# An early-fusion layer of patches and text: the head on inputs laid out beforehand, expert weights split in place, batch 0 picked in two steps, the softmax ahead of the experts

## The chip, the cores and the metric

The kernel runs on one core of a Trainium2 chip. The metric is the device time of one execution in microseconds (us). A core has TensorE (PE, with its weight loads apart as PEld), VectorE (DVE), ScalarE (ACT), GpSimd (POOL) and the queue engine SyncE (SP), which all run their own instruction streams and meet at semaphores. 16 DMA engines move data between memory and SBUF.

## What is computed

```python
patches = [x and four copies shifted by 8 pixels]          # 32 x 36 patches of 3840 values
h = ((patches - mu) * rsqrt(var + eps) * gamma + beta) @ W.T + b     # W: 192 x 3840
h = concatenate([h, txt], axis=1)                          # 32 x 164 x 192
n = layernorm(h)
k, v, q = n @ w_key.T, n @ w_value.T, n @ w_query.T        # 8 heads of 64
k0, v0, g0 = k[0], v[0], sigmoid(n @ w_gate.T)[0]          # of batch 0 alone
for t in sequence:                                         # retrieved, then written
    out_t = q_t @ fw;  fw = 0.95 * fw + 0.1 * g0_t * outer(k0_t, v0_t)
h = h + n + out @ w_out.T
n = layernorm(h);  xf = rmsnorm(n) * norm_w                # 5248 tokens
p = softmax(xf @ router_w.T);  top 2 of 8 experts
y = sum over them of p_e * down_e(silu(gate_e xf) * (up_e xf))       # 384 wide
h = h + n + y
```

All arrays are float32. An image is 96 x 96 with three channels, so it has 6 x 6 patches.

## The kernel before

The kernel is one block in which each engine's queue is written out by hand in Python; semaphores are named after what is ready (wait_ge). A tile is 4 sequence positions of 32 batches, 128 rows; there are 41 tiles, 9 of them patches, and the residual hres holds all of them in SBUF. The program has these stages.

*Preparation.* SP's queue (L358) loads W, beta, gamma, the image in 12 pieces of 32 partitions, and the text. Attention weights come through ScalarE's queue (L434). TensorE transposes w_out (L690), forms for each head the products gT (key by query weights) and hT (value by output weights) (L701), 192 columns each, and transposes W (L717). VectorE multiplies W by gamma and folds columns that shifted copies share. GpSimd copies image rows into strips, TensorE transposes them (L738), VectorE copies them to imgT (L1048).

*Patches* (L750). Nine patches, each 24 products of 128 x 128 by 193 columns; the 193rd column gives the sum of the pixels. An fp32 product is two instructions on TensorE in the trace. ScalarE's squares (L471, L474), before all patches in its queue, give the variance; VectorE finishes each token (L1072).

*Batch 0.* Its normed row x0T comes from a round trip through DMA; the gates, keys and values of all heads follow (L773, L794), with evictions L523 and L1142; the gates reach their partitions by eight small DMAs.

*Chunk loop.* Eleven chunks of 16 positions (4 tiles). Per chunk TensorE makes the transposes turn (L782), rows (L802, L804), scores (L814), the read-out of the state (L820) and of the chunk itself (L824), and the state's update (L835). ScalarE copies the transposed tokens out (xT_out, L518), computes std2 (L545), and norm2 (L555 to L559), which writes the rows that are scattered. VectorE adds the residual, takes the statistics and top 2 and gives each token a place. GpSimd scatters each tile twice (L662) to the place of its expert in memory. Between them stand *units* of expert weights: TensorE transposes a piece (L852, L853, L858), ScalarE writes its high half rounded (high, L572 and L576), VectorE the rest (low, L1238 and L1244). 20 units stand in the loop, 24 after it. At the end VectorE computes the table of slots (L1266 to L1288).

*Experts.* 89 slots of 128 rows each: SP loads the rows of a slot (L413) when all scatters are done, TensorE runs a pipeline of transposes and products, GpSimd scatters each result.

*Tail.* Results come back in groups of four tiles (L346), ScalarE takes the softmax's exp (L630), VectorE adds two results per tile (L1343), stores leave by both queues (L356).

```python
def unit(n):                       # before: 12 down units, then 32 of gate and up
    k = n - NE * FC // 2
    return None if k < 0 else (k // 4, k // 2 % 2, k % 2)
for n in range(LOOP_UNITS, UNITS): # VectorE, after the table
    low(n)
```

## Time and profile before

| what | us |
|---|---|
| median of 3 runs | 672.92 (671.53 to 672.93) |
| profiled execution, its own time | 671.68 |
| its span | 669.9 |
| preparation and patches | 0 to 164.1 |
| batch 0, to the chunk loop | 164.1 to 207.2 |
| chunk loop, table, last units | 207.2 to 338.0 |
| experts | 338.0 to 625.9 |
| tail | 625.9 to 669.9 |

The rows further down are from the views of the trace: windows give each engine's busy time in a stretch with the number of instructions in brackets, PEclk the clock granted to TensorE as a share of the full 2.4 GHz (0.50 is 1.2 GHz), and GB/s what the DMA engines moved. A timeline's row gives the start, the duration, the engine, the line and operation, then output<-input, and in brackets the idle time ahead of it and what released it. The ends of products are modelled, so that the spacing of starts tells more than a duration.

### The profile page before, as it was taken

How to read it: one execution, taken by the hardware profiler on the slowest of the kernel's cores; microseconds unless marked ns; L12 is line 12 of the kernel's file. 1: busy time of each engine (PE TensorE's matmuls, PEld its weight loads, DVE VectorE, ACT ScalarE, POOL GpSimd, SP SyncE). 2: the span in 40 equal slices, each digit the busy share in tenths (PEclk: the TensorE clock that was granted, in tenths of full speed). 3: DMA queues.
4: the chain of work that ended last, by engine and by line, in shares of the span. 5: the costliest groups of instructions: out<-in, count | busy, mean ns of one | idle time of the engine just before them, and what ended most of it. 6: DMA issues, size and time to landing. Idle time of an engine off the chain costs nothing.

```text
span 669.9 us, 13234 instructions
## 1 busy us (share of the span) xinstructions
PE 541.2 (81%) x3330; PEld 500.7 (75%) x3331; DVE 402.7 (60%) x1310; ACT 305.2 (46%) x718; POOL 198.5 (30%) x293
## 2 busy tenths in 40 slices
PE   0079998997589999984679999999999999999000
PEld 0067688997487877873379999999999999999000
DVE  4590617666414777788956566566566566565197
ACT  0035992222623667767644444444444444444100
POOL 0001510000000577777403333333333333333100
PEclk9999998999599999998789999999999999999655
DMA  9999700000861122222312222222222222221695
GB/s 201 236 170 187 139 0 1 7 1 0 204 187 42 54 81 78 79 79 85 106 38 78 69 73 79 69 74 78 69 77 74 69 79 72 69 80 48 214 371 155
DMA packets 85236, 64.87 MB, mean 97 GB/s; under 512 B 42501, under 2 KB 81897, under 8 KB 84825
## 3 DMA queue, kind: packets, MB, share of 16 engines
q1 hardware_dynamic: 67160, 39.93, 26.8%
q0 software_dynamic: 8208, 16.95, 7.2%
...
q14 instruction: 15, 0.11, 0.1%
...
## 4 chain that ended last, share of the span: by engine, by line
PE 69%; DVE 14%; ACT 7%; DMA 4%; issue 3%; ACTq 2%; POOL 0%; POOLq 0%; SPq 0%; DVEq 0%
PE pair L750 9%; PE bank L946 5%; PE bank L942 5%; PE bank L944 5%; PE bank L945 5%; PE bank L943 5%; PE bank L953 4%; PE pair L820 4%; DVE hres L1343 4%; ACT sqjunk L471 4%; PE bank L962 4%; PE pair L962 4%; DMA bet<-in_L_tok_ln_beta 3%; PE pair L931 3%; PE bank L701 3%
## 5 line engine op out<-in xcount | busy, mean ns | idle before, releaser
L662 POOL DMA_INDIRECT disp<-xf,posu x82 | 79.8, 973 | 154.3 <-ACT xf L559 130.2
L674 POOL DMA_INDIRECT ydram<-ysb,dnow x89 | 87.3, 981 | 69.4 <-POOL dnow L671 67.1
L1308 DVE TENSOR_TENSOR hh<-sg,bank 128x384 f32<-128x384 f32 x89 | 49.3, 554 | 93.4 <-ACT sg L613 93.4
L613 ACT ACTIVATE sg<-bank 128x384 f32<-128x384 f32 x89 | 43.7, 491 | 111.5 <-PE bank L946 111.5
L750 PE MATMUL pair<-wcT,imgT 128*128 128x193 f32 x432 | 73.4, 331 | 3.8 <-DVE tmp L1063 3.8
L750 PEld LDWEIGHTS pair<-wcT,imgT 128*128 128x128 f32 x432 | 72.4, 193 | 4.1 <-issue 4.1
L942 PE MATMUL bank<-wa,xh 128*128 x178 | 67.7, 380 | 0.0
L946 PE MATMUL bank<-wa,xl 128*128 x178 | 60.3, 339 | 0.0
L944 PE MATMUL bank<-wa,xl 128*128 x178 | 60.2, 338 | 0.0
L945 PE MATMUL bank<-wa,xh 128*128 x178 | 60.0, 337 | 0.0
L943 PE MATMUL bank<-wa,xh 128*128 x178 | 60.0, 337 | 0.0
L671 POOL COPY dnow<-dest 128x1 uint32 (+1 forms) x89 | 16.5, 186 | 123.9 <-DVE ysb L1318 123.9
L1311 DVE TENSOR_TENSOR htl<-bank,hth 128x384 fp32r<-128x384 f32 x89 | 48.9, 550 | 0.9 <-ACT hth L616 0.9
L962 PE MATMUL pair<-wd,hth 128*128 x135 | 44.5, 380 | 0.4 <-DVE htl L1311 0.4
L953 PE MATMUL bank<-ident,hh 128*128 128x128 f32 x267 | 43.6, 272 | 0.6 <-DVE htl L1311 0.6
L962 PE MATMUL bank<-wd,hth 128*128 x132 | 43.6, 380 | 0.0
L616 ACT CAST hth<-bank 128x384 fp32r<-128x384 f32 x89 | 42.4, 476 | 0.8 <-PE bank L953 0.8
L931 PE MATMUL pair<-ident,xs 128*128 128x128 f32 x178 | 34.4, 275 | 4.0 <-DVE wa L1244 3.0
L953 PEld LDWEIGHTS bank<-ident,hh 128*128 128x128 f32 x267 | 34.6, 140 | 3.8 <-DVE hh L1308 0.8
L1304 DVE TENSOR_TENSOR xl<-pair,xh 128x256 fp32r<-128x256 f32 x89 | 37.2, 418 | 0.4 <-ACT xh L610 0.4
L652 POOL COPY strip<-img 128x512 f32<-128x512 f32 x24 | 13.7, 606 | 77.5 <-DMA img<-in_x 62.8
L820 PE MATMUL pair<-nst,xT 96*128 96x208 f32 x164 | 36.3, 343 | 0.0
...
## 6 DMA issues: line engine op xcount, KB each, us to landing
...
```

Of the source, the lines that this page charges most:

```text
L662: pool.indirect_dma_start(disp, bass.IndirectOffsetOnAxis(ap=posu[c % XBUF][:, 2 * j + k:2 * j + k + 1], axis=0), xfd[c % XBUF][:, j, :], None
L674: pool.indirect_dma_start(ydram, bass.IndirectOffsetOnAxis(ap=dnow[b][:], axis=0), ysb[b][:], None).then_inc(s_ys[b], 16)
L750: ins = pe.matmul(bank[5 + p % 2][:, 0:193], imgT[:, 2 * i + dr, j + s, c, :], wcT[:, k, :], start=(k == 0), stop=(k == 23))
L820: pe.matmul(o, xT[c % 2][:, m, P * j:P * j + P], nst[c % 2][:, m, :], start=(m == 0), stop=False)
L931: ins = pe.transpose(bank[5][:, P * m:P * m + P], xs[b][:, P * m:P * m + P], ident[:])
L942: pe.matmul(acc, xh[o][:, 0:P], high, start=True, stop=False)
L943: pe.matmul(acc, xh[o][:, 0:P], low, start=False, stop=False)
L944: pe.matmul(acc, xl[o][:, 0:P], high, start=False, stop=False)
L945: pe.matmul(acc, xh[o][:, P:2 * P], rest, start=False, stop=False)
L946: ins = pe.matmul(acc, xl[o][:, P:2 * P], rest, start=False, stop=True)
L953: ins = pe.transpose(bank[4][:, P * c:P * c + P], hh[b][:, P * c:P * c + P], ident[:])
L962: pe.matmul(bank[6 + o][:, 0:2 * D], hth[o][:, P * c:P * c + P], wd[:, both], start=(c == 0), stop=False)
```

## The change

All inputs are laid out by numpy before the launch: the pixels as imgT wants them, a second copy of them in four horizontal bands for the squares, W cut into 30 pieces of 128 x 192, the attention weights transposed, the text by partitions, gate, up and down weights transposed. No transposes of weights or images are left on TensorE, no strips on GpSimd, no border zeroes and no head products. VectorE multiplies the 24 pieces of W by gamma and adds six shared ones. TensorE multiplies all 30 by gamma and beta to get two row sums (L711), spreads them over the partitions (L733), and runs the patches over four banks (L727). The squares move between the patches on ScalarE's queue. Bands 2 and 3 reuse the buffers of 0 and 1.

Keys and values of batch 0 come in two steps. First the projections of the text positions (L742, between patches 7 and 8) and their products with query or output weights (L757). Then the patches' positions are picked from hres by products with a one-hot selection scaled by the rstd (L807, L811), projected, and multiplied (L765). The gates are picked on VectorE.

There are 4 down units in the head and 24 of gate and up in the loop, in 22 turns, none after it. The loaded piece lies where its low half will: ScalarE writes the high half from it, VectorE subtracts. The second norm of chunk 0 moves to the end of chunk 0 in ScalarE's queue. The softmax stands ahead of the experts. Results lie in memory by partition, and the first loads of the tail have 1, 1 and 2 tiles.

```diff
+LOADS = (0, 1, 2, 4, 8, 12, 16, 20, 24, 28, 32, 36, 40, 41)
...
+        def turn_units(t):
+
+            n = UNITS - DOWN_UNITS
+            return range(DOWN_UNITS + max(0, t - 1) * n // (TURNS - 1), DOWN_UNITS + t * n // (TURNS - 1))
...
-            sp.dma_start(wraw[:], W.rearrange("(m p) f -> p m f", p=DH)).then_inc(s_wraw, 16)
-            sp.dma_start(bet[:], beta.partition_broadcast(DH)).then_inc(s_bet, 16)
-            sp.dma_start(gam[:], gamma.partition_broadcast(DH)).then_inc(s_gam, 16)
...
+                sp.dma_start(wraw[:, 15 * i:15 * i + 15, :], W[:, 15 * i:15 * i + 15, :]).then_inc(s_wraw[i], 16)
+            for i in range(2):
+                sp.dma_start(imgT[:, 2 * i:2 * i + 2], pixels[:, 2 * i:2 * i + 2]).then_inc(s_img[i], 16)
+            for i in range(2):
+                sp.dma_start(band[i][:], bands[:, i]).then_inc(s_band[i], 16)
+            sp.dma_start(imgT[:, 4:6], pixels[:, 4:6]).then_inc(s_img[2], 16)
+            sp.dma_start(hres3[:, PTILES:TILES, :], text).then_inc(s_txt, 16)
...
+            sp.wait_ge(s_row, 1)
...
+                sp.dma_start(x0[32 * q:32 * q + 32, :], text[32 * q]).then_inc(s_x0, 16)
+            sp.dma_start(imgT[:, 6:8], pixels[:, 6:8]).then_inc(s_img[3], 16)
+            sp.dma_start(aw[:], attn_w).then_inc(s_attw, 16)
+            for i in range(2):
+                sp.wait_ge(s_sq, 12 + 9 * i)
+                sp.dma_start(band[i][:], bands[:, 2 + i]).then_inc(s_band[2 + i], 16)
+                if i == 0:
+                    sp.dma_start(wd4[:, :, 1, :].bitcast(F32), down_w).then_inc(s_rawd, 16)
+
...
+            for e in range(NE):
+                sp.dma_start(wa5[:, e, 1].bitcast(F32), gu_w[0:P, e]).then_inc(s_rawm[e], 16)
+            sp.wait_ge(s_kv, 4 * NH)
+            for r in range(2 * NE):
+                if r >= RING:
+                    sp.wait_ge(s_lo, DOWN_UNITS + 3 * ((r - RING) // 2) + (r - RING) % 2 + 2)
+                for half in range(2):
+                    sp.dma_start(ring[r % RING][64 * half:64 * half + 64, :], gu_w[P:D, r // 2, r % 2]).then_inc(s_rawr[r % RING], 16)
...
+                lines = (0, 1) if i == 0 else (i + 1,)
+                if j == 0:
+                    for b in lines:
+                        act.wait_ge(s_band[b], 16)
+                for b in lines:
+                    square(sqjunk[:], band[b % 2][:, :, :, 16 * j:16 * j + 32], 12 * j + 3 * b + 1)
+                square(sqjunk[:, :, 0:8, 0:16], band[i % 2][:, :, 8:16, 16 * j + 8:16 * j + 24], 12 * j + 3 * i + 2)
+                square(sqjunk[:, :, 0:8, 0:16], band[(i + 1) % 2][:, :, 0:8, 16 * j + 8:16 * j + 24], 12 * j + 3 * i + 3)
+
...
+                    if k == 0:
+                        act.wait_ge(s_rawm[e], 16)
+                        ins = nc.scalar.activation(wa5[:, e, 0], wa5[:, e, 1].bitcast(F32), ACT.Copy, scale=nwab[:, 0:1])
+                    else:
+                        r = 2 * e + k - 1
+                        act.wait_ge(s_rawr[r % RING], 32 * (r // RING + 1))
+                        ins = nc.scalar.activation(wa5[:, e, 2, k - 1], ring[r % RING][:], ACT.Copy, scale=nwab[:, 1:2])
...
                 if c + 1 < CHUNKS:
                     xT_out(c + 1, 0)
-                if c + 1 < CHUNKS:
-                    high(2 * c)
+                for n in turn_units(2 * c):
+                    high(n)
                 if c + 1 < CHUNKS and nt(c + 1) > 2:
                     xT_out(c + 1, 1)
-                if c:
+                if c > 1:
                     norm2(c - 1)
                 if c + 1 < CHUNKS:
                     state_out(c + 1)
-                    high(2 * c + 1)
+                for n in turn_units(2 * c + 1):
+                    high(n)
                 if c + 2 < CHUNKS:
                     rows(c + 2)
                 if c:
                     add_norm2(c - 1)
                 std2(c)
+                if c == 0:
+                    norm2(0)
             norm2(CHUNKS - 1)
             add_norm2(CHUNKS - 1)
...
+            act.wait_ge(s_w, 1)
+            nc.scalar.activation(top8[:, 0:8 * TILES], top8[:, 0:8 * TILES], ACT.Exp).then_inc(s_exp, 1)
+            nc.scalar.preload_act_table_set("silu_and_others")
...
+            pe.wait_ge(s_par, 16)
+            for k in range(WCOLS):
+                if k % 15 == 0:
+                    pe.wait_ge(s_wraw[k // 15], 16)
+                pe.matmul(bank[4][0:2, 0:D], gb[:, k, :], wraw[:, k, :], start=(k == 0), stop=False)
+            pe.wait_ge(s_cst, 16)
+            pe.wait_ge(s_bias, 16)
+            pe.matmul(bank[4][0:2, 0:D], cst[0:1, C_ONE:C_ONE + 2], biasr[:], start=False, stop=True).then_inc(s_row, 1)
 
...
+                if p >= 4:
+                    pe.wait_ge(s_patout, p - 3)
...
+            for p in range(1, 7):
+                patch(p)
+            pe.wait_ge(s_x0n, 1)
+            for m in range(2):
+                ins = pe.transpose(bank[2][0:DH, P * m:P * m + P], x0n[:, DH * m:DH * m + DH], ident[:])
+            ins.then_inc(s_x0t, 1)
+            patch(7)
...
+            def pick(tiles):
+                a, n = tiles[0], len(tiles)
+                pe.matmul(x0sel[:, :, a:a + n, :], onesf[:, 0:DH], selr[:, 1, a:a + n].unsqueeze(1).to_broadcast([P, 2, n, TQ]),
+                          start=True, stop=False)
+                for t in tiles:
+                    for m in range(2):
+                        ins = pe.matmul(x0sel[:, m, t, :], hres3[:, t, DH * m:DH * m + DH], selr[:, 0, t, :],
+                                        start=False, stop=(t == tiles[-1] and m == 1))
+                return ins
+
+            pe.wait_ge(s_rsel, 1)
...
+            text_kv(1, 0)
+            pe.wait_ge(s_head, 1)
+            pe.wait_ge(s_patout, 9)
+            for which in range(2):
+                for hp in range(4):
+                    ins = project(head_bank[which][:, HEAD_S * hp:HEAD_S * hp + HEAD_S], (wkT, wvT)[which], hp, 0, HEAD_S)
+                ins.then_inc(s_k0, 1)
+            text_kv(1, 1)
+            for m in range(2):
+                ins = pe.matmul(bank[3][:, 0:SPAD], wgR[:, m, :], x0T[:, m, :], start=(m == 0), stop=(m == 1))
+            ins.then_inc(s_g8, 1)
+            turn(0, 0)
+            text_kv(1, 2)
+            text_kv(1, 3)
+            for which in range(2):
+                pe.wait_ge((s_k0head, s_v0head)[which], 1)
+                pe.wait_ge(s_vvout, 6 + 2 * which)
+                for hp in range(4):
+                    head_kv(which, hp)
 
...
+            def low(n):
+                v.wait_ge(s_hi, n + 1)
+                if unit(n) is None:
+                    raw = wd4[:, 6 * n:6 * n + 6, 1, :]
+                    ins = v.tensor_tensor(raw, raw.bitcast(F32), wd4[:, 6 * n:6 * n + 6, 0, :].bitcast(F32), ALU.subtract)
+                else:
+                    e, k = unit(n)
+                    if k == 0:
+                        raw = wa5[:, e, 1]
+                        ins = v.scalar_tensor_tensor(out=raw, in0=raw.bitcast(F32), scalar=nwab[:, 0:1],
+                                                     in1=wa5[:, e, 0].bitcast(F32), op0=ALU.mult, op1=ALU.subtract)
+                    else:
+                        both = wa5[64:P, e, 2, k - 1, :]
+                        ins = v.scalar_tensor_tensor(out=both, in0=ring[(2 * e + k - 1) % RING][64:P, :], scalar=nwab[64:P, 1:2],
+                                                     in1=both.bitcast(F32), op0=ALU.mult, op1=ALU.subtract)
+                ins.then_inc(s_lo, 1)
+
+            for p in range(9):
...
+            t4 = top8[:].rearrange("p (c j e) -> p c j e", j=4, e=8)
+            t3 = top8[:, 0:8 * TILES].rearrange("p (n e) -> p n e", e=8)
+            st.link(v.tensor_tensor(t4, t4, rs[:, :, 1, :].unsqueeze(3).to_broadcast([P, CHUNKS, 4, 8]), ALU.mult))
+            st.link(v.tensor_copy(esum[:], t3[:, :, 0]))
+            v.tensor_tensor(t3, t3, esum[:].unsqueeze(2).to_broadcast([P, TILES, 8]), ALU.subtract).then_inc(s_w, 1)
+            v.wait_ge(s_exp, 1)
+            st.link(v.tensor_reduce(esum[:], t3, AX.X, ALU.add))
+            st.link(v.reciprocal(esum[:], esum[:]))
+            st.link(v.tensor_tensor(wts[:].rearrange("p (n k) -> p n k", k=2), t3[:, :, 0:2],
+                                    esum[:].unsqueeze(2).to_broadcast([P, TILES, 2]), ALU.mult))
...
-    c[:, C_DEST:C_DEST + TILES] = 2 * (P * np.arange(TILES)[None] + p[:, None])
+    c[:, C_DEST:C_DEST + TILES] = 2 * (np.arange(TILES)[None] + TILES * p[:, None])
...
+        "pixels": quads.reshape(P, CH, 8, 8, 4, 16).transpose(5, 3, 2, 4, 1, 0).reshape(P, 8, 4, CH, P),
+        "bands": quads.reshape(P, CH, 4, 16, 64).transpose(0, 2, 1, 3, 4),
+        "text": txt.reshape(B, TILES - PTILES, TQ, D).transpose(2, 0, 1, 3).reshape(P, TILES - PTILES, D),
+        "patch_w": pieces(inputs["L0_tok_W"]),
```

TensorE's queue in the preparation before, behind the transposes of w_out: the last head product and the first transposes of W (wraw), which go on for nine more such groups.

```order
L701 MATMUL bank<-woT,wv 96x192 [waits product_out]
L701 MATMUL bank<-woT,wv 96x192
L717 MATMUL bank<-ident,wraw 128x96 [waits product_out,patch_weights_ready]
L717 MATMUL bank<-ident,wraw 128x96 x7
L717 MATMUL bank<-ident,wraw 128x96 [waits wT_out]
L717 MATMUL bank<-ident,wraw 128x96 x3
```

TensorE's queue from its start now, with row sums (of wraw, the pieces of W) and the first patches:

```order
L711 MATMUL bank<-wraw,qpar 2x192 [waits patch_weights_in0,params_in]
L711 MATMUL bank<-wraw,qpar 2x192 x14
L711 MATMUL bank<-wraw,qpar 2x192 [waits patch_weights_in1]
L711 MATMUL bank<-wraw,qpar 2x192 x14
L714 MATMUL bank<-biasr,cst 2x192 [waits bias_in,consts_in]
L727 MATMUL bank<-wcT,imgT 128x193 [waits pixels_in1,pixels_in0,patch_weights_ready]
L727 MATMUL bank<-wcT,imgT 128x193 x23
L733 MATMUL bank<-rowsb,onesf 128x384 [waits rows_masked]
L738 MATMUL bank<-ident,rw_66 96x8 [waits router_centred,pool_constants]
L738 MATMUL bank<-ident,rw_66 96x8
L727 MATMUL bank<-wcT,imgT 128x193 x24
L727 MATMUL pair<-wcT,imgT 128x193 x24
```

The transposes and products are gone; 30 products and the bias stand ahead of patch 0, and the spreading of the row sums and the router's transposes behind it.

ScalarE's queue around the ends of chunks 0 and 1 before (xT is a turn's copy, sq the std2, xf what norm2 writes, wd and wa high halves, nst the state, crow and arow the rows):

```order
L545 ACTIVATE sq<-mv_138,cst 128x4 [waits var2]
L546 ACTIVATE sq<-mv_138,cst 128x4
L518 COPY xT_150<-bank 96x2x256 [waits state_mm,xT_mm]
L572 CAST wd<-bank 128x2x192 [waits expertT_mm]
L518 COPY xT_150<-bank 96x2x256 [waits state_mm,xT_mm]
L555 COPY xf_86<-cst 128x4x2 [waits rstd2]
L557 COPY xf_86<-idxf 128x4
L559 ACTIVATE xf_86<-hres,bb,rs 128x192 x4
L539 COPY nst_143<-bank 96x2x200 [waits state_mm]
L572 CAST wd<-bank 128x2x192 [waits expertT_mm]
```

And now:

```order
L586 ACTIVATE sq<-mv_128,cst 128x4 [waits var2]
L587 ACTIVATE sq<-mv_128,cst 128x4
L596 COPY xf_78<-cst 128x4x2 [waits rstd2]
L598 COPY xf_78<-idxf 128x4
L600 ACTIVATE xf_78<-hres,bb,rs 128x192 x4
L560 COPY xT_140<-bank 96x2x256 [waits state_mm,xT_mm]
L501 ACTIVATE wa<-ring_62,qpar 128x384 [waits raw_rest_in0]
L560 COPY xT_140<-bank 96x2x256 [waits state_mm,xT_mm]
```

norm2(0) went ahead of both xT copies that TensorE's turns of chunk 2 wait for, and a high half from a ring buffer stands between them.

VectorE at the end of the table before:

```order
L1286 TENSOR_SCALAR slotf<-slotf 128x91 [waits dve_steps]
L1287 CAST tab<-slotf 128x91 [waits dve_steps]
L1288 CAST tab<-slotf 128x91
L1244 SCALAR_TENSOR_TENSOR wa<-bank,nwab,wa 128x384 [waits expert_high,dve_steps]
L1244 SCALAR_TENSOR_TENSOR wa<-bank,nwab,wa 64x384 [waits expert_high]
```

And now (top holds the logits, wts the weights):

```order
L1330 CAST tab<-slotf 128x91
L1335 TENSOR_TENSOR top_136<-top_136,rs 128x352 [waits dve_steps]
L1336 COPY esum<-top_136 128x41 [waits dve_steps]
L1337 TENSOR_TENSOR top_136<-top_136,esum 128x328 [waits dve_steps]
L1339 TENSOR_REDUCE esum<-top_136 128x41 [waits softmax_exp]
L1340 RECIPROCAL esum<-esum 128x41 [waits dve_steps]
L1341 TENSOR_TENSOR wts<-top_136,esum 128x82 [waits dve_steps]
L1349 SCALAR_TENSOR_TENSOR dest<-xs_155,slotf 128x1 [waits xsT_mm,dve_steps]
```

The 24 low halves are gone from there, and the softmax's six operations, with a wait for ScalarE's exp, stand ahead of the first slot's operations.

## Rows read from the trace of the kernel before

**Rows 1.** Windows by stage: from:to, length, busy time of each engine, PEclk, DMA, GB/s.

```profile
0.00:103.10 103.10, 59.17 (x299) 49.53 (x300) 46.85 (x82) 50.02 (x68) 14.90 (x33) 1.00 0.87 152
103.10:164.10 61.00, 60.35 (x360) 59.22 (x360) 39.13 (x172) 14.55 (x37) 0.00 (x0) 0.97 0.01 3
164.10:207.20 43.10, 29.85 (x172) 26.25 (x172) 14.73 (x62) 16.70 (x38) 0.00 (x0) 0.84 0.62 168
207.20:338.00 130.80, 110.79 (x632) 88.54 (x632) 102.71 (x461) 87.02 (x217) 79.82 (x82) 0.95 0.22 72
338.00:625.90 287.90, 281.04 (x1869) 277.15 (x1869) 169.12 (x448) 135.19 (x357) 103.81 (x178) 0.99 0.25 71
625.90:669.90 44.00, 0.00 (x0) 0.00 (x0) 30.12 (x85) 1.76 (x2) 0.00 (x0) 0.50 0.84 275
```

**Rows 2.** Windows of 2 us, loading W and loading results.

```profile
14.00:16.00 2.00, 0.00 (x0) 0.00 (x0) 0.00 (x0) 0.00 (x0) 0.00 (x0) 1.00 1.05 223
...
638.00:640.00 2.00, 0.00 (x0) 0.00 (x0) 1.97 (x7) 0.00 (x0) 0.00 (x0) 0.50 1.06 373
```

**Rows 3.** TensorE's timeline: head products at the start, and the patches.

```profile
41.63 1.16 PE L701 MATMUL bank<-wq,wk 64*96 64x192 f32 x3
42.59 1.16 PE L701 MATMUL bank<-woT,wv 64*96 64x192 f32 x3
...
124.56 39.53 PE L750 MATMUL pair<-wcT,imgT 128*128 128x193 f32 x240
```

**Rows 4.** Groups by line: count, then busy us, mean ns of one, idle before.

```profile
L471 ACT ACTIVATE sqjunk<-img 128x3072 bf16<-128x3072 f32 x9 | 24.9, 2764 | 0.3
...
L996 DVE TENSOR_TENSOR wq<-wq,wqm 128x768 f32<-128x768 f32 x1 | 1.0, 959 | 0.0
```

**Rows 5.** TensorE: a group of head products (timeline), and the rows' narrow products (lines).

```profile
187.73 1.36 PE L794 MATMUL pair<-x0T,hT 96*96 96x176 f32 x8
...
L804 PE MATMUL bank<-rwsc,valsT 96*128 96x8 f32 x44 | 5.9, 243 | 0.0
```

**Rows 6.** Timelines of the loop: GpSimd, VectorE, ScalarE, SP's queue, TensorE.

```profile
222.45 1.14 POOL L662 DMA_INDIRECT disp<-xf,posu  x1 [129.28 <-ACT xf L559]
...
316.59 1.25 POOL L662 DMA_INDIRECT disp<-xf,posu  x1 [0.30 <-issue]
...
318.14 1.60 POOL L662 DMA_INDIRECT disp<-xf,posu  x1 [0.30 <-issue]
...
326.37 0.96 POOL L662 DMA_INDIRECT disp<-xf,posu  x1 [0.30 <-issue]
...
316.09 0.92 DVE L1277 TENSOR_TENSOR tabf<-cst,ct 128x728 f32<-128x728 f32 x1
...
317.99 0.92 DVE L1280 TENSOR_TENSOR tabf<-tabf,ct 128x728 f32<-128x728 f32 x1
...
321.58 15.47 DVE L1244 SCALAR_TENSOR_TENSOR wa<-bank,nwab,wa 128x384 fp32r<-128x384 f32 x24
...
220.32 0.58 ACT L518 COPY xT<-bank 96x512 f32<-96x512 f32 x1 [1.86 <-PE bank L782]
...
221.00 1.86 ACT L559 ACTIVATE xf<-hres,bb,rs 128x192 f32<-128x192 f32 x4
...
329.85 0.37 SPq L413 DMA_DIRECT2D xs<-disp  x1
...
338.01 0.41 PE L931 MATMUL pair<-ident,xs 128*128 128x128 f32 x2 [2.97 <-DVE wa L1244]
```

**Rows 7.** Timelines of the tail: ScalarE's queue and VectorE.

```profile
625.85 7.89 ACTq L346 DMA_DIRECT2D yall<-ydram  x5
...
636.84 29.70 DVE L1343 SCALAR_TENSOR_TENSOR hres<-yall,wts,hres 128x192 f32<-128x192 f32 x82
```

**Rows 8.** Windows late in the chunk loop, columns as in the first group.

```profile
297.00:307.00 10.00, 7.57 (x49) 6.81 (x46) 8.55 (x43) 6.61 (x18) 7.56 (x9) 1.00 0.23 79
307.00:317.00 10.00, 3.93 (x17) 3.08 (x17) 7.87 (x42) 7.01 (x21) 7.56 (x9) 0.73 0.23 79
```

859 lines of the change are left out of this document (417 added, 442 removed).

## The prediction

> **What bounds the kernel now.** The windows by stage come first [rows 1]. The experts' stage, 338.0 to 625.9, takes 287.9 us with TensorE busy 281.0, and the change touches no instruction in it. The time to be won lies around it: 207.2 us before the chunk loop, 130.8 from its start to the first expert slot, 44.0 behind the last slot. The profiled execution took 671.68 us for a span of 669.9, so 1.8 us lie outside the span; the median of the runs shown, 672.92, is 0.2% above it.
>
> In the first 103.1 us TensorE is busy 59.2, though the transfers run at 152 GB/s on average: the loads come in narrow shapes, and behind them come the folding of W, the head products and the transposes. The patches then run one after another, busy 60.35 of 61.00. In the 43.1 us after them TensorE is busy 29.9. In the loop GpSimd issues its 82 scatters in an unbroken row, the first at 222.45, the last at 326.37 [rows 6], so one every (326.37 - 222.45 - 0.93)/81 = 1.27 us, the 0.93 being two stretched ones; eight of them make 10.1 us a chunk. The last scatter ends at 327.33, the first slot's load is issued at 329.85, but TensorE begins at 338.01, since 24 units of expert weights (15.47 us of VectorE) stand after the table [rows 6]. In the tail the loads are issued at 625.85 and the first addition runs at 636.84 [rows 7].
>
> **Head, to the loop's start (call it L; 207.2 before).** *Loads.* W goes out first on SP's queue, two pieces of 1.47 MB over 128 partitions with 11.5 KB in a row. Bounds on their rate: 223 GB/s, the old W over 96 partitions, and 373, the results over 128 partitions [rows 2]. I take 370, the row with the same partitions and long rows. With 3.2 us until data flows (my estimate from the first window), piece 0 is there at 7.2, piece 1 at 11.2, pixels for the first three patches at 19.2.
> *Row sums.* TensorE starts cold with 30 matmuls of 192 columns, two instructions each. At the start of the old kernel's work such an instruction took 0.96/3 = 0.32 us, against 39.53/240 = 0.165 for 193 columns in mid-run [rows 3]; so these run at 1.2 GHz, the lower of the two clocks. Price: 30 x 0.656 = 19.7, at the other clock 9.9. They are ahead of patch 0 in TensorE's queue, so it waits for them, not for the weights: VectorE's fold (four operations of 128 x 1152, each 1.5 x 0.96 by the row of 768 [rows 4], and twelve of 192 columns) is ready at 17.7. Patch 0 starts at 7.2 + 19.7 + 1 = 28.
> *Patches.* 9 x 48 x 0.165 = 71.1; the first partly at the low clock +2; row spread, x0's two transposes and queueing +1.5; the 32 projection instructions between patches 7 and 8 +3.5 at 0.11 each. They end at 106. Gone are 96 image and 48 W transposes, the products and the strips. The squares, of which the larger pieces alone took 24.9 us ahead of the patches [rows 4], now lie beside them: one patch costs ScalarE at most two pieces of 1536 elements and two of 384, 0.9 ns an element by 2764/3072, 3.5 us under 7.9.
> *To L.* Key products over the text 7.0 (32 instructions x 0.11 = 3.5, and as much for the squares, projections and additions still queued on ScalarE and VectorE); picks of batch 0, 22 matmuls = 44 instructions x 0.135 by the eight-column row, 5.9 [rows 5]; value products 4.0; head projections 4.3; gate 0.6; turns 0.9; 32 head products, 64 instructions, 7.7 (0.12 each, under the 0.135 of the eight-column row since their spans overlap; 1.36/8 = 0.17 for 176 columns is the upper bound [rows 5]); evictions, rows and scores 4.6. Sum 35, against 43.1 before, with the transfer of the gate through memory and x0's round trip gone. **L = 141**, 66 us earlier.
>
> **Loop, L to the first slot.** Before, the first scatter stood at L + 15.2 and the slot's data could have been used at L + 125.3: the last scatter's end and 5.2 more. The 24 units kept it to L + 130.8; moving them into the loop gives at most 5.5 back. Three things take from it.
> *The second norm of chunk 0* now stands ahead of the copies xT(2,0) and xT(2,1). Before, it stood behind them, and ScalarE waited 1.86 us for the second at 220.32, so norm 0 began at 221.00 [rows 6]. Its four activations (1.86) and their wait for VectorE now stand ahead of a copy that TensorE's turn(2,1) waits for. Chunk 0 scatters some 2.4 us sooner, chunk 1's chain comes some 3.5 later. Bounds -2.4 and +3.5; I take +1.9, what GpSimd is starved once it has used its lead.
> *Splitting units.* The low halves (8 of 128 x 768, 16 of 64 x 384) took one operand from PSUM; now both come from SBUF. In this trace the two table operations with both big operands in SBUF, 316.09 and 317.99, are exactly those under which scatters took 1.25 and 1.60 us instead of 0.96 [rows 6]; the reductions between them stretched none. A 0.96 us operation that starts anywhere in the 1.27 us period holds up the next scatter by some 0.3 on average, one of 0.5 us by 0.1: 8 x 0.3 + 16 x 0.1 = **+4.0**. Bounds 0 and their whole length, 8 x 0.96 + 16 x 0.5 = 15.7; the two stretches measured (0.29 and 0.64) hold me near the low end. The Trainium skill, "SBUF — State Buffer", section "Who interferes with whom", says that a VectorE operation with both inputs in SBUF locks GpSimd's reads out for as long as it lasts. By that rule these units cost GpSimd time in a stage that GpSimd bounds; the trace agrees in the two scatters, and by the rule at its hardest the loop would end some 12 us later than in my sum.
> *TensorE* loses its expert transposes; its 10.3 us a chunk fall to some 8.3, hidden under GpSimd's 10.1. The softmax (under 3 us on VectorE, its exp on ScalarE) hides behind the last scatters, which end 5.6 us after the table. If that cover went, it would cost those 3.
> Sum: 125.3 + 1.9 + 4.0 = **131.2**.
>
> **Experts** 287.9, as before. **Tail.** A first load of one tile lets additions start at +3.2 instead of +11.0 [rows 7]: landing about 2 us, issue the rest. Gone from the front are the exp's table load and the softmax's four operations. Then 82 additions 29.3, waits for the growing pieces 1.5, the last store 3.9: 37.9, take **38**. It can't go under 12.1 MB / 373 GB/s = 32.4 [rows 2].
>
> **Sum:** 141 + 131.2 + 287.9 + 38 = 598.1, and 1.8 outside: **600**.
>
> **Rivals.**
> *A, the loads stay slow.* For it: 223 GB/s at 14 to 16 and 152 over the head. Against it: those rows are 96 partitions and runs of 224 bytes. At 225 GB/s the third band, queued behind text, pixels and attention weights, lands at 88; patch 3's squares wait for it, and patch 6 waits for one of four banks. L = 153, time 613.
> *B, TensorE starts fast.* The row sums take 9.9, patch 0 waits for its weights and pixels at 20: 592. Against it: the first rows behind an idle stretch ran at 1.2 GHz [rows 3].
> *C, the loop is free:* no stretched scatters and norm 0 early, the slot at L + 126: 595.
> *D, the clock falls in the loop.* With the expert transposes gone TensorE idles. It held the full clock at 76% busy (297 to 307), and fell to 0.73 at 39% (307 to 317) [rows 8]. At some 80% it should hold; where it doesn't, a chunk's 8.3 us become 16 and pass GpSimd's 10.1 until it rises again. I price it at 1 us a chunk: 610.
> *Slower than before: the loads throttle everything.* 19 MB must come in ahead of L, of which 69 us of work can't be covered: L = 69 + 19/r. It decides at L = 213, r = 132 GB/s, where the time reaches 673. The head's average is 152, with descriptors fifty times shorter, so it is remote: 675 to 690.
> *The change doesn't do what it says:* small first loads and the early softmax bring nothing, since a hidden DMA limits the tail: that is 605 and lies in the range; that all of it brings nothing has 1 in 100.
>
> **How the numbers follow.** Forecast 0.54 (its own range 592 to 608), A 0.15, B 0.11, C 0.10, D 0.07, slower 0.02, nothing 0.01. The low end, 585, is B with C and 2 us of head; the high end, 616, is A with a few us of locked scatters. About 0.2% is what a measurement of this kernel can tell from no change. Faster 0.97, same 0.01, slower 0.02.
>
> **What would show it.** First rows on TensorE: 0.33 us an instruction from about 7 us on; patch 0 at 28; the patches 7.9 apart to 106 with no wait for squares; the loop's first rows at 141. GpSimd's first scatter at L + 13, its last at L + 125, with some twenty stretched ones under the low halves. First slot at L + 131. First addition 3 us behind the last store. I am wrong if wraw lands after 10, if a patch waits for a band, if ScalarE's queue holds up the key products by more than 4 us, or if DMA is over 95% busy in the tail while additions wait.

## The result, and the profile after

The changed kernel takes 593.44 us (median of 4 runs, 592.90 to 593.84) against 672.76 for the kernel before (4 runs), a ratio of 0.882 (95% interval 0.881 to 0.884). The forecast was 600. The profiled execution took 593.84 for a span of 592.1. Its windows by stage, in the same columns and with the same cuts as [rows 1], with one more cut at the first patch:

```profile
0.00:20.63 20.63, 12.70 (x63) 5.80 (x64) 9.79 (x19) 0.00 (x0) 1.36 (x10) 1.00 0.92 373
20.63:103.47 82.84, 78.65 (x470) 77.53 (x470) 53.39 (x230) 54.51 (x116) 0.00 (x0) 0.96 0.50 189
103.47:133.66 30.19, 28.38 (x242) 25.25 (x241) 11.34 (x41) 12.84 (x30) 0.00 (x0) 0.72 0.37 124
133.66:265.59 131.93, 88.47 (x493) 75.00 (x492) 96.92 (x447) 81.45 (x202) 81.94 (x82) 0.87 0.30 91
265.59:554.40 288.81, 282.15 (x1869) 278.18 (x1869) 167.98 (x445) 133.49 (x356) 104.15 (x178) 0.98 0.26 71
554.40:592.10 37.70, 0.00 (x0) 0.00 (x0) 29.04 (x82) 0.00 (x0) 0.00 (x0) 0.50 0.88 321
```

The chunk loop starts at L = 133.66 instead of 207.2: that is 73.5 of the 77.8 us that the span lost. The loop to the first slot takes 131.9 (130.8 before), so its end brought nothing, the experts 288.8 (287.9), the tail 37.7 (44.0). What the prediction rests on in the head is in these rows of TensorE, VectorE and ScalarE (timeline: start, busy, engine, line, operation, count, idle before and what ended it):

```profile
7.79 12.29 PE L711 MATMUL bank<-wraw,qpar 128*2 128x192 f32 x60 [7.79 <-DMA wraw<-in_patch_w]
20.63 8.14 PE L727 MATMUL bank<-wcT,imgT 128*128 128x193 f32 x48
89.39 6.28 PE L742 MATMUL bank<-x0T,aw 96*128 96x128 f32 x32 [4.19 <-DVE x0T L1161]
113.32 7.06 PE L742 MATMUL bank<-x0T,aw 96*128 96x48 f32 x32
...
10.54 0.19 DVE L994 COPY wcT<-cst 128x24 f32<-128x24 f32 x1 [10.54 <-DMA cst<-in_consts]
81.20 2.63 DVE L1116 TENSOR_TENSOR wd<-wd 128x1152 fp32r<-128x1152 f32 x2 [6.27 <-ACT wd L492]
...
77.11 1.48 ACT L464 ACTIVATE sqjunk<-band 128x1536 bf16<-128x1536 f32 x1 [2.70 <-DMA band<-in_bands]
...
80.02 2.21 ACT L492 CAST wd<-wd 128x1152 fp32r<-128x1152 f32 x2
```

The row sums (L711) begin 7.8 us in and take 12.3: the first 16 of their 60 instructions start 0.32 us apart, the others 0.16. The fold waits until 10.5 for a copy of constants ahead of it in VectorE's queue (L994), and ends together with the sums. TensorE idles 4.2 us for x0T (L1161), behind the casts of the down units (L492, L1116). Those casts stand behind squares for which ScalarE itself waits 2.70 us, until the fourth band has landed (L464, 77.11). The projections after it run at the lower clock:

```profile
7.00:13.00 6.00, 5.21 (x18) 2.21 (x19) 2.46 (x3) 0.00 (x0) 0.00 (x0) 1.00 1.02 429
13.00:20.00 7.00, 7.00 (x44) 3.50 (x42) 6.86 (x15) 0.00 (x0) 0.00 (x0) 1.00 1.01 427
89.00:95.50 6.50, 6.11 (x32) 6.14 (x33) 4.81 (x10) 2.77 (x4) 0.00 (x0) 0.57 0.01 3
112.00:124.00 12.00, 12.00 (x60) 10.87 (x62) 2.77 (x8) 2.32 (x7) 0.00 (x0) 0.50 0.15 58
```

These are windows in the head (columns as above; PEclk, DMA share and GB/s last). The loads run at 427 to 429 GB/s, where 370 was taken from [rows 2]. The Trainium skill, "DMA: Bandwidth & Descriptors", section "Where 436 GB/s comes from", gives 435 GB/s as the ceiling of the ports into SBUF and some 358 for what memory gives a core, and says that the second binds transfers from memory. The trace lies just under the first figure and above the second, and the measurement decides. The last line shows 12 us between patches and loop at 0.50 of the clock, the lower of the two levels.

In the loop, of GpSimd, ScalarE, TensorE and VectorE:

```profile
147.61 1.12 POOL L683 DMA_INDIRECT disp<-xf,posu  x1 [145.43 <-ACT xf L600]
162.78 0.96 POOL L683 DMA_INDIRECT disp<-xf,posu  x1 [5.19 <-ACT xf L600]
181.64 1.34 POOL L683 DMA_INDIRECT disp<-xf,posu  x1 [0.31 <-issue]
...
146.15 1.86 ACT L600 ACTIVATE xf<-hres,bb,rs 128x192 f32<-128x192 f32 x4
147.91 0.56 ACT L560 COPY xT<-bank 96x512 f32<-96x512 f32 x1
...
161.47 1.86 ACT L600 ACTIVATE xf<-hres,bb,rs 128x192 f32<-128x192 f32 x4
...
148.62 0.61 PE L779 MATMUL bank<-ident,hres 128*96 128x128 f32 x4 [2.89 <-ACT xT L560]
...
265.59 0.69 PE L946 MATMUL pair<-ident,xs 128*128 128x128 f32 x2 [20.40 <-DMA xs<-disp]
...
144.52 1.01 DVE L1121 SCALAR_TENSOR_TENSOR wa<-wa,qpar 128x768 fp32r<-128x768 f32 x1
181.13 1.01 DVE L1121 SCALAR_TENSOR_TENSOR wa<-wa,qpar 128x768 fp32r<-128x768 f32 x1
```

GpSimd scatters chunk 0 and then stands for 5.19 us, where it stood for nothing before [rows 6]: chunk 1's rows come late. Norm 0 (L600) runs ahead of the copy xT (L560), and TensorE's turn waits 2.89 us for that copy. One scatter, at 181.64, takes 1.34 us under a low half on VectorE (L1121, 181.13).

In the tail (SP's queue and VectorE) the loads go out at 554.40 and the first addition runs 3.41 us later, against 10.99 in [rows 7]:

```profile
554.40 3.34 SPq L366 DMA_DIRECT2D yall<-ydram  x7
...
557.81 1.53 DVE L1383 SCALAR_TENSOR_TENSOR hres<-yall,wts,hres 128x192 f32<-128x192 f32 x4 [6.85 <-DMA yall<-ydram]
```

### The profile page after: what moved, and what is told of

Same layout as the page of the kernel before. It is cut to its first block, busy times and chain, and to the rows that moved or that the text cites. A ratio compares the mean times of both kernels' runs of the same rounds, so it can differ in the third digit from the quotient of the medians.

```text
span 592.1 us, 12735 instructions
## 1 busy us (share of the span) xinstructions
PE 490.3 (83%) x3132; PEld 461.8 (78%) x3133; DVE 368.5 (62%) x1263; ACT 282.3 (48%) x703; POOL 187.5 (32%) x270
## 4 chain that ended last, share of the span: by engine, by line
PE 61%; DVE 18%; DMA 10%; ACT 5%; issue 3%; POOL 2%; SPq 1%; DVEq 0%; POOLq 0%
DMA hres<-in_text 6%; PE bank L961 5%; PE bank L959 5%; PE bank L958 5%; PE bank L957 5%; PE bank L960 5%; PE bank L968 5%; DVE hres L1383 4%; PE bank L977 4%; PE pair L977 4%; PE pair L863 4%; PE pair L946 3%; PE pair L867 3%; ACT sqjunk L464 2%; PE bank L742 2%
## 5 line engine op out<-in xcount | busy, mean ns | idle before, releaser
L683 POOL DMA_INDIRECT disp<-xf,posu x82 | 81.9, 999 | 176.4 <-ACT xf L600 151.5
L692 POOL COPY dnow<-dest 128x1 uint32 (+1 forms) x89 | 16.6, 186 | 119.0 <-DVE ysb L1368 118.9
L946 PE MATMUL pair<-ident,xs 128*128 128x128 f32 x178 | 34.9, 278 | 21.4 <-DMA xs<-disp 20.4
L727 PE MATMUL bank<-wcT,imgT 128*128 128x193 f32 x240 | 40.2, 327 | 0.1
L727 PEld LDWEIGHTS bank<-wcT,imgT 128*128 128x128 f32 x240 | 39.3, 189 | 0.6 <-DVE zrow L1012 0.5
L642 ACT CAST xh<-pair 128x256 fp32r<-128x256 f32 x89 | 33.5, 376 | 11.2 <-PE pair L946 11.2
L863 PE MATMUL pair<-nst,xT 96*128 96x208 f32 x164 | 38.0, 356 | 0.2 <-ACT nst L580 0.2
L946 PEld LDWEIGHTS pair<-ident,xs 128*128 128x128 f32 x178 | 20.8, 143 | 22.0 <-DMA xs<-disp 21.9
```

The source lines that it names most:

```text
L683: pool.indirect_dma_start(disp, bass.IndirectOffsetOnAxis(ap=posu[c % XBUF][:, 2 * j + k:2 * j + k + 1], axis=0), xfd[c % XBUF][:, j, :], None
L727: ins = pe.matmul(bank[PATCH_BANK[p % 4]][:, 0:193], imgT[:, 2 * i + dr, j + s, c, :], wcT[:, k, :], start=(k == 0), stop=(k == 23))
L863: pe.matmul(o, xT[c % 2][:, m, P * j:P * j + P], nst[c % 2][:, m, :], start=(m == 0), stop=False)
L946: ins = pe.transpose(bank[5][:, P * m:P * m + P], xs[b][:, P * m:P * m + P], ident[:])
```

## The experiments

The total came near the forecast, but four terms looked off: the start, the stretch between patches and loop, norm 0, and the locked scatters. Twelve runs followed on three chips. On the chip of e1 to e4 and on that of the four g kernels every kernel was slower, the one before too (717.4 and 718.1); the extra time lies in the chunk loop, where VectorE and ScalarE stand still together for several us. In g0, the changed kernel itself, the timeline of the two has rows such as these, in which the profile names nothing on the core as releaser:

```profile
186.46 0.22 DVE L1271 TENSOR_TENSOR ohm<-oh,pair 128x64 f32<-128x64 f32 x1 [4.13 <-remote]
186.62 0.58 ACT L560 COPY xT<-bank 96x512 f32<-96x512 f32 x1 [3.36 <-remote]
```

So from those chips I read the head, the first two chunks and the tail, and compare kernels of one chip. The third chip (before 673.15), that of e5, e6, h1 and h2, has none of it. All of them, from their traces ("+" counts from L; scatter 9 is chunk 1's first; the column of times gives the number of executions in brackets):

| kernel | time (n) / before on that chip | patch 0 | patches end | L | scatter 1 | scatter 9 | L to slot | slot to tail | tail |
|---|---|---|---|---|---|---|---|---|---|
| after | 593.44 (4) / 672.76 | 20.63 | 103.54 | 133.66 | +13.95 | +29.1 | 131.93 | 288.81 | 37.7 |
| e1 | 632.53 (4) / 717.37 | 21.36 | 104.14 | 134.35 | +14.69 | +28.3 | 169.53 | 289.15 | 37.7 |
| e2 | 631.23 (4) / 717.37 | 21.71 | 97.73 | 132.63 | +13.96 | +32.2 | 169.57 | 289.14 | 37.6 |
| e3 | 632.73 (1) | 21.5 | 100.71 | 134.33 | +13.15 | +31.6 | 170.33 | 288.34 | 37.9 |
| e4 | 636.32 (1) | 21.83 | 102.21 | 136.26 | +15.94 | +34.6 | 171.83 | 288.76 | 37.8 |
| g0 | 642.11 (2) / 718.05 | 21.49 | 100.54 | 140.61 | +15.92 | +34.5 | 172.04 | 288.65 | 37.6 |
| g1 | 627.49 (2) / 718.05 | 21.81 | 100.42 | 134.00 | +14.68 | +26.0 | 167.54 | 289.38 | 37.4 |
| g3 | 631.56 (1) | 21.52 | 103.51 | 133.62 | +13.15 | +31.4 | 169.55 | 288.99 | 37.6 |
| g9 | 629.79 (1) | 18.69 | 102.4 | 132.64 | +13.95 | +31.9 | 169.45 | 288.45 | 37.5 |
| e5 | 605.54 (1) | 21.61 | 100.65 | 140.72 | +16.10 | +31.7 | 134.98 | 288.58 | 39.5 |
| e6 | 595.05 (1) | 21.43 | 100.53 | 132.62 | +13.96 | +29.1 | 132.61 | 288.44 | 39.6 |
| h1 | 586.61 (3) / 673.15 | 18.71 | 94.70 | 132.02 | +14.69 | +25.4 | 127.22 | 287.89 | 37.8 |
| h2 | 591.71 (4) / 673.15 | 18.73 | 94.72 | 142.37 | +16.84 | +27.5 | 128.48 | 288.41 | 37.7 |

**Norm 0 behind the copies: e1, and g1 on the other chip.** The edit of both:

```diff
-                if c > 1:
+                if c:
                     norm2(c - 1)
...
-                if c == 0:
-                    norm2(0)
```

> The changed kernel with one part undone: the second norm of chunk 0 stands again behind the two xT copies of chunk 2, as in the kernel before. Theory: in the changed kernel GpSimd is starved for 4.9 us at 157.6 to 162.8 since ScalarE's four activations and their wait for VectorE hold up TensorE's turn of chunk 2 (idle 2.89 us at 148.6). Then this gap goes, chunk 0's first scatter comes some 2 us later (L + 16), chunk 1's no later than L + 26, and the first slot starts 3 us sooner: L + 129, span 589. Rival: the gap comes from the units of expert weights, for whose high half VectorE waits 3.18 us at 149.1 ahead of its residual. Then the gap stays about as long, and the first slot starts at L + 132 or later, span 592.

> The second norm of chunk 0 back behind the two xT copies, beside a control on the same chip. Theory as before: TensorE's wait of 2.9 us and most of GpSimd's 4.9 us without work in chunk 1 go, the first scatter comes 1 to 2 us later, and the first slot starts 2 to 3 us sooner after L than in the control. Rival: the units hold VectorE up just as long, and the first slot comes no sooner than in the control.

In e1 the first scatter comes 0.73 us later than in e2 of the same chip, and chunk 1's first one at L + 28.3 instead of L + 32.2, not at the L + 26 that was expected: one of the standstills (3.09 us of VectorE) lies ahead of it. In g1 the row of scatters goes nearly straight on into chunk 1:

```profile
160.01 0.96 POOL L681 DMA_INDIRECT disp<-xf,posu  x1 [0.69 <-issue]
```

That is L + 26.0, against L + 31.9 in g9 and L + 34.5 in g0, the kernels of that chip that keep norm 0 ahead. So the mechanism stands. In e1's total nothing of it is to be seen (L to slot 169.53, against 169.57 in e2), since the standstills of that chip use up any lead; in g1 it is 1.9 us against g9 and 4.5 against g0, but g9 and g0, which have the same loop, differ by 2.6 among themselves. The size is read from h1 below, which has other edits too; no kernel with this edit alone ran on a chip without standstills.

**The down units one patch later: e2.**

```diff
-                if 4 < p < 7:
+                if 5 < p < 8:
                     ...
-                        high(2 * (p - 5) + n)
+                        high(2 * (p - 6) + n)
```

(and the same for the low halves on VectorE).

> The changed kernel with its four down units one patch later in ScalarE's and VectorE's queues, so that the copy x0T on VectorE has none of them ahead. Theory: TensorE's wait of 4.19 us ahead of the projections at 89.4 comes from the low halves, which VectorE waits for (6.27 us) ahead of patch 5's and 6's work; with it goes the fall of the clock to 0.57 in the projections (6.3 us where 3.5 would do). Patches end at 97 instead of 103.5, and L is 6 to 7 us earlier: span 586. Rival: the fourth band, which ScalarE waits for until 77.1, sets x0T's time, or the units now hold up the picks: at most 1 us is gained, span 591.

The wait for x0T and the fall of the clock behind it go: the patches end at 97.7, six us earlier than in after and three to six than in the others of its chip. But L is 132.6, only some 1.7 earlier than e1 and e3, and e6, with the head of after, has the same 132.6; so a gain at L isn't clear of the spread. Behind the patches TensorE now waits there (timeline):

```profile
101.88 0.53 PE L757 MATMUL bank<-k0T,aw 64*96 64x128 f32 x1 [3.10 <-ACT keysT L537]
```

ScalarE and VectorE have the last patch's evictions and the last down units ahead of the keys, and keysT is late; the products behind it start 0.21 us apart, twice the 0.11 of those before the wait. The cause of the first wait is confirmed, and the gain was mostly or wholly handed to the next wait. The other traces say the same without an edit: in e3, g0, g1, e5 and e6, whose heads are that of after, the projections took 3.81 us at the full clock instead of 6.28, the patches ended at 100.4 to 100.7, and the wait for keysT was 2.5 us instead of 0.4.

**Low halves of one column: e3, and g3 on the other chip.** Both leave out all but one column of each low half, so the experts work with wrong weights.

```diff
-                        ins = v.scalar_tensor_tensor(out=raw, in0=raw.bitcast(F32), scalar=nwab[:, 0:1],
+                        ins = v.scalar_tensor_tensor(out=raw[:, 0, 0:1], in0=raw[:, 0, 0:1].bitcast(F32), scalar=nwab[:, 0:1],
```

> The changed kernel, in which the 24 low halves of gate and up are computed for one column only; the rest of them is left as loaded. It prices what VectorE's operations with both operands in SBUF cost GpSimd's scatters. The prediction had 4.0 us for it. The trace of the changed kernel shows four stretched scatters ahead of the table's (0.38, 0.66, 0.36 and 0.09 us over 0.96), 1.5 us in all. By that these four stretches go, those under the table's two operations and the softmax stay (0.64, 0.63, 0.17), and the first scatter comes 1 us sooner since the first low half stood ahead of chunk 0's scaling: first slot at L + 129.5 instead of L + 131.9. By the prediction's price it would be L + 127.

> The 24 low halves of gate and up for one column only (the rest stays as loaded), beside a control on the same chip. By the four stretches that the trace shows ahead of the table: scatters stretched by 1.5 us less than in the control, first scatter 1 us sooner, first slot 2 to 3 us sooner after L. By the prediction's price of 4.0 us for the stretches: 5 us sooner.

The first scatter comes at L + 13.15 in both, 0.8 earlier than in after, e2, e6 and g9, which have full low halves: a whole 1.01 us one (L1121 at 144.52, above) stood ahead of norm 0's scales. Time over 0.96 us, summed over all scatters, is 1.01 in g3 and 1.33 in g0; none of g3's lies under a low half, and of g0's only 0.2. In after, four scatters of the 82 are longer under low halves, by 0.38, 0.66, 0.36 and 0.09: 1.5 us, where 24 such operations run. In the four runs of the third chip it is 6 to 9 scatters and 1.7 to 2.3 us. What the low halves cost the loop in all can't be told from e3 and g3, since both ran where engines stand still (169.55 and 170.33, inside the spread of the others).

**Fewer narrow products in batch 0's picks: e4.** It leaves out all but the last tile's selections, so keys and values of batch 0 are wrong.

```diff
-                for t in tiles:
+                for t in tiles[-1:]:
```

> The changed kernel without 14 of the 18 narrow products that pick batch 0's patches out of hres (the last tile of each pick stays), so keys, values and gates of the patch positions are wrong. The trace shows TensorE's clock at 0.50 from 109 to 124.6 though it is busy all the time, with the head projections at 7.06 us. Theory: products of four columns make the clock fall, and without them it stays at 1.00 to the loop: 4.7 us of picks and some 7 us of slow clock go, L = 122, span 580. Rival: the clock falls for the gaps at 104.6 and 108.9 or since the projections before ran in a cold stretch; then only the 4.7 us go, L = 129, span 587.

```profile
106.00:109.00 3.00, 1.42 (x17) 1.33 (x16) 1.98 (x14) 2.01 (x4) 0.00 (x0) 1.00 0.96 358
...
130.00:133.00 3.00, 3.00 (x6) 1.59 (x7) 0.00 (x0) 0.64 (x2) 0.00 (x0) 0.50 0.46 132
```

The windows (columns as above) show TensorE idle for half of the time in which the picks stood, and the clock down at 130, when it had long risen in after. L is 136.3, not earlier. So the clock falls there without most of the narrow products too; with them gone there is idle time in their place. Whether it would hold with neither, the run doesn't tell.

**Loads of four tiles first: e5. Softmax behind the experts: e6.**

```diff
-LOADS = (0, 1, 2, 4, 8, 12, 16, 20, 24, 28, 32, 36, 40, 41)
+LOADS = (0, 4, 8, 12, 16, 20, 24, 28, 32, 36, 40, 41)
```

> The changed kernel with its first tail load of four tiles again instead of 1, 1 and 2. Theory: the first addition waits for 786 KB instead of 197 KB while the other queue's load runs beside it: 3.4 us from the tail's start become 5.5 to 6, the additions behind wait no more, and the tail takes 39 to 40 us instead of 37.7. Rival: the tail's end is set by the transfers, which go on at 370 GB/s either way: 37.7.

> The changed kernel with the softmax behind the experts again. Theory: ScalarE issues its six loads (2.9 us), loads the exp's table (1.28) and takes the exp (0.48), then VectorE's reduction, reciprocal and product follow (1.2): first addition at 6.4 us from the tail's start instead of 3.4, tail 40.5 instead of 37.7. The loop's end is unchanged (the softmax was behind the last scatters). Rival: the additions catch up, since later ones wait for loads anyway: tail under 38.5.

In e6 exp moves behind load_results on ScalarE, and the softmax's operations stand on VectorE between the experts and the additions. First e5, then e6, timelines of the tail:

```profile
564.28 2.96 SPq L366 DMA_DIRECT2D yall<-ydram  x6
...
570.35 4.74 DVE L1383 SCALAR_TENSOR_TENSOR hres<-yall,wts,hres 128x192 f32<-128x192 f32 x13 [9.50 <-DMA yall<-ydram]
```

```profile
553.67 3.50 SPq L366 DMA_DIRECT2D yall<-ydram  x7
...
556.83 1.28 ACT L660 ACT_TABLE_LOAD   x1 [7.60 <-issue]
...
559.89 5.53 DVE L1383 SCALAR_TENSOR_TENSOR hres<-yall,wts,hres 128x192 f32<-128x192 f32 x15
```

The first addition starts 6.07 us behind the issue with loads of four, 6.22 with the softmax there, 3.41 in after. The tails are 39.5, 39.6 and 37.7: 1.8 and 1.9 us each, less than the 2.7 and 2.8 by which the start moves, since additions that start early wait later for the growing pieces (0.79 us in after). Either one alone holds the start back to +6, so each gives its gain only with the other; the kernel with neither wasn't run. What brings the tail from 44.0 to 39.5 wasn't tried apart (the results lie in memory in another layout).

**A warm start: g9.** TensorE multiplies ones for 16 products before W lands, and the copy of constants moves behind the fold.

```diff
+            pe.wait_ge(s_pool, 1)
+            for k in range(16):
+                pe.matmul(bank[3][:, 0:P], onesf[:], onesf[:], start=True, stop=True)
```

> The changed kernel with 16 products of ones on TensorE from 1 us on, ahead of the row sums (their result is used nowhere), and with VectorE's copy that waits for the constants (10.5 us) behind its folding of W instead of ahead of it. Theory: both the row sums (12.3 us, 18 instructions at half clock) and the fold (ready at 20.35) end together and set patch 0; with the clock up from the start the sums take 9.9 us and end at 17.9, and the fold, from 8 us on, ends at 18: patch 0 at 18.2 instead of 20.6, and the whole 2.4 us shorter. Rival: the pixels or the second piece of W come later than 18, or the half clock of the start isn't cured by these products: patch 0 at 20 or later.

```profile
1.04 5.23 PE L709 MATMUL bank<-onesf 128*128 128x128 f32 x32 [1.04 <-POOL onesf L665]
7.56 9.91 PE L714 MATMUL bank<-wraw,qpar 128*2 128x192 f32 x60 [1.28 <-DMA qpar<-in_params]
18.69 3.52 PE L730 MATMUL bank<-wcT,imgT 128*128 128x193 f32 x20 [0.81 <-DMA imgT<-in_pixels]
```

The sums take 9.91 us, 0.165 an instruction from the first on, and patch 0 comes at 18.7, two to three us earlier; now it waits for pixels. The price of the sums was a matter of what TensorE did before them. Little of the gain reaches L (132.6, against 133.6 to 134.0 in g1 and g3): the copy x0T stands at 88.15 as in g0 (88.14), since the band still lands at 76.6, and TensorE waits 5.65 us for it instead of 1.13.

**All of it, g0, h1 and h2.** g0 is the changed kernel again. h1 has the edits of e1, e2 and g9, and 34 products of ones behind the product of the counts, to keep the clock up to the first slot. h2 adds 13 more: 4 before the second half of the key products, five between the tiles of the picks, and 4 ahead of the later picks.

> The changed kernel itself, as the measure for the others of this chip: on the chip of the first experiments the chunk loop of every kernel, the one before too, was some 38 us longer than in the first comparison (171 us from L to the first slot), with VectorE and ScalarE idle at the same time for 4 to 15 us. Here the first slot is expected at L + 132 if the chip is like the first one, at L + 170 if it is like the second.

> The changed kernel with what the experiments so far point to, together: second norm of chunk 0 back, down units one patch later, fold ahead of the wait for constants, 16 products of ones ahead of the row sums, and 34 products of 256 columns on TensorE behind the counts, in the 20 us in which it would idle ahead of the first slot (their results are used nowhere). By the parts measured: patch 0 at 18.7 (20.6 or 21.5 without), patches over at 95, L = 130 (133.7 without), first slot at L + 129 on a chip without the stalls in the loop and L + 167 with them, and the experts' stage 287.9 instead of 288.8 because it starts at full clock. Sum with the stalls: 130 + 167 + 288 + 37.7 = 623, against 630 of the changed kernel by its windows. Rival: the parts don't add, since the projections' end only moves the waits behind it: L = 132 or later, and the span is that of the second norm alone, 628.

> The kernel before it (h1_all), and 13 more products of ones, 128 columns each, between the picks of batch 0 and ahead of two waits behind the patches (their results are used nowhere; 2.9 us at full clock). Theory: TensorE's clock falls to 0.50 from 101 or 109 on because the stretch behind the patches has waits and narrow products; where that stretch is filled, the clock stays at 1.00 to the loop, the head projections take 3.6 us instead of 7.0, and L is 4 to 5 us earlier than in h1_all, fillers counted. Rival: the clock falls as before, and the fillers cost 2 to 5 us on top: L later than in h1_all.

h1 takes 586.61 us (ratio to before 0.870, interval 0.865 to 0.875), 6.8 us or 1.2% under the changed kernel. Its stages, and its ScalarE and GpSimd in the first chunks:

```profile
0.00:18.71 18.71, 15.81 (x94) 10.43 (x96) 10.46 (x20) 0.00 (x0) 1.36 (x10) 1.00 0.91 367
18.71:94.70 75.99, 75.99 (x472) 75.14 (x472) 47.84 (x219) 53.04 (x115) 0.00 (x0) 1.00 0.57 217
94.70:132.02 37.32, 30.90 (x240) 27.68 (x241) 16.32 (x51) 14.28 (x32) 0.00 (x0) 0.68 0.29 100
132.02:259.24 127.22, 103.43 (x562) 87.83 (x560) 96.77 (x447) 81.39 (x202) 82.57 (x82) 0.95 0.31 94
259.24:547.13 287.89, 281.22 (x1869) 277.49 (x1869) 168.01 (x445) 133.11 (x356) 103.64 (x178) 0.99 0.26 71
...
142.24 0.56 ACT L560 COPY xT<-bank 96x512 f32<-96x512 f32 x1
...
155.07 1.86 ACT L600 ACTIVATE xf<-hres,bb,rs 128x192 f32<-128x192 f32 x4
...
157.41 0.96 POOL L681 DMA_INDIRECT disp<-xf,posu  x1 [0.30 <-issue]
```

The copy xT stands at L + 10.2 (142.24), where after has it at L + 14.3 behind norm 0; chunk 1's norm starts at L + 23.1 (155.07) instead of L + 27.8 (161.47), for a scatter at 157.41, and no scatter of the 82 waits. From after to h1 the span falls by 7.2: patch 0 earlier by 1.9, patches shorter by 6.9, patches to L longer by 7.1, loop shorter by 4.7, experts by 0.9. The loop's 4.7 are 6.3 of starvation gone, less 0.7 for the later first scatter, 0.6 for more stretched ones and 0.2 between the last scatter and the slot. The experts' 0.9 goes with the clock, which is at 0.50 for the first 6.5 us of the stage in after and for 3.4 in h1: the stage is back at the 287.9 of [rows 1].

Of the 7.1 that came back 5.3 are this wait (h1; 0.43 in after). The rest goes with the clock, at 0.50 for 23.9 us there instead of 17.1. h2's windows show why its fillers didn't help:

```profile
101.50 0.53 PE L758 MATMUL bank<-k0T,aw 64*96 64x128 f32 x1 [5.75 <-ACT keysT L537]
```

```profile
97.00:100.00 3.00, 0.00 (x0) 0.00 (x0) 2.89 (x7) 0.00 (x0) 0.00 (x0) 0.83 0.97 370
100.00:103.00 3.00, 1.26 (x12) 1.26 (x14) 2.75 (x12) 1.33 (x6) 0.00 (x0) 0.50 1.03 402
130.00:133.00 3.00, 3.00 (x42) 3.00 (x40) 0.00 (x0) 0.85 (x2) 0.00 (x0) 0.50 0.00 0
```

TensorE does nothing at 97 to 100, ahead of the picks, since the first fillers stood elsewhere; the clock falls there already, and everything behind it, fillers too, runs at half of it past 133. L is 142.4, ten us later than in h1. (This is h2's profiled execution, which took 598.8; the median is 591.7, so in its other executions L was probably less late.)

## Why the prediction was right, and where not

**Start: too dear by 7.4.** Patch 0 was put at 28 and came at 20.6. The step that failed is the price of the 30 row sums, 19.7 us at the lower clock throughout; they took 12.3. The row of [rows 3] behind it shows how the first products run, not how long that lasts: here 16 instructions ran at 0.32 and 44 at 0.16. This is half of rival B, to which I had given 0.11. A smaller part is the loads: 427 GB/s, not 370. That TensorE's queue and not the weights would set patch 0 was only half right: the fold, held by the constants until 10.5, ended at the same moment; in the nine other runs with this start it ended later, TensorE waited 0.9 to 2.3 us for it, and patch 0 came at 21.4 to 21.8. g9 shows both.

**Patches: 82.9 for 78.** No product waits for a band, as predicted, but ScalarE's squares do (2.1 us at 54.2, 2.7 at 77.1), and the second wait pushes the casts behind it, which the prediction had not counted. The 32 projection instructions were priced at 3.5 with no wait ahead of them; the down units in VectorE's and ScalarE's queues weren't counted: 4.2 us of waiting for x0T, the stage's only idle time, and 6.3 for the projections at the lower clock. e2 shows that without the units there is no wait, late band or not. They end at 103.5, for 106. The 3.5 was right for a projection that stays at the full clock: 3.81 in five other runs of this head.

**To L: 30.2 for 35.** The picks took 6.0 (5.9 was taken). The backlog of 3.5 us that I put on the key products over the text was 0.4 in after (they took 2.7 for 7.0), but came with 2.5 us in the five runs named at e2 and with 3.1 to 5.8 in e2, h1 and h2, where the patches before it run faster. I had no term for the clock, which stands at 0.50 from 108 to 125 and makes the head projections 7.1 for 4.3.

**Loop: 131.9 for 131.2, by two errors against each other.** Norm 0: +1.9 was taken, with a bound of +3.5. Starvation is 6.3, the first scatter comes 1.3 earlier (not 2.4), together +5.0, outside the bound. The bound took ScalarE's time and its wait as the delay, once; but chunk 1's whole chain hangs on the copy, through TensorE's turn, and its norm comes 4.8 later; the lead that could take this up is only 1.0 us, since the scatter follows norm 1 by 2.3 us in h1 (155.07 and 157.41), where it stands behind other scatters, and by 1.3 in after, where it doesn't. The loop with norm 0 behind, in h1, is 4.7 shorter (131.93 and 127.22, chips without standstills), stretched scatters included. Splitting units: +4.0 was taken, 1.5 came as stretched scatters, near the low end of the bounds. The Trainium skill, "SBUF — State Buffer", section "Who interferes with whom", lets each such operation lock GpSimd's reads out for its whole length; the trace agrees in that the stretched scatters lie under them, but only 4 scatters were lengthened beside 24 of them (6 to 9 on the third chip), and the 12 us that the rule at its hardest would have added didn't come. Rival D did not come about: the clock over the loop was 0.87, but it stood at 1.00 from 173.1 to 237.9, with TensorE busy 84% of that time (some 80% was taken), and was low mainly behind it, where TensorE has little left to do; the terms above account for the loop without it. The softmax lies hidden, as predicted.

**Experts and tail.** 288.8 for 287.9: TensorE idles 20.4 us before the first slot and starts cold, 0.9 us, for which there was no term. Tail 37.7 for 38, first addition at +3.4 for +3.2.

The sum, 598.1, and the span, 592.1, differ by 6.0: start 7.4 and the way to L 4.8 too dear, patches 4.8 too cheap, loop, experts and tail together 1.3 too cheap (0.7, 0.9 and -0.3), which is 6.1 with rounding. The total was partly luck: errors of 5 to 7 us fell on both sides. With the start put right and nothing else, the forecast would have been near 593, as rival B's 592; but with the patches put right as well it would have been near 597 again. The measured 593.4 lies nearer to B's 592 than to 600, and at the low end of the forecast's own range. Of the signs that were named, patch 0 at 28, the loop's first rows at 141 and twenty stretched scatters did not show; the slot at L + 131 and the first addition at 3 us did.

**What stays open.** No run takes the new inputs of the head apart, so how the 73.5 us divide among loads, transposes and products is read from windows alone. The same code from patches to loop takes 30 to 40 us: L is 132.6 to 134.4 in the six kernels with after's head (after, e1, e3, g1, g3, e6), and 140.6 and 140.7 in g0 and e5, which differ from after in nothing before the tail. Windows of g0 and of after:

```profile
102.00:106.00 4.00, 1.87 (x16) 1.68 (x16) 3.68 (x15) 1.91 (x7) 0.00 (x0) 0.71 0.96 321
138.00:142.00 4.00, 4.00 (x17) 3.58 (x16) 0.69 (x1) 1.22 (x3) 0.00 (x0) 0.50 0.00 0
```

```profile
102.00:106.00 4.00, 3.57 (x42) 3.06 (x40) 3.37 (x13) 1.54 (x7) 0.00 (x0) 1.00 0.34 75
126.00:130.00 4.00, 3.41 (x69) 3.13 (x69) 1.61 (x6) 1.44 (x3) 0.00 (x0) 1.00 0.02 4
```

In g0 TensorE is busy 1.87 of 4 us at 102 to 106, and the clock falls there and stays down until about 145; in after it falls at 108 and rises at 125. Why it stays down so much longer, with TensorE busy throughout, no run tells. h2's fillers were misplaced, so what fillers in the idle 96 to 101.5 of h1 would bring is open too. The standstills with a releaser called "remote" on two chips are described, not explained.
